# Second attention of a vision tower: q and k projected two images ahead among the scores, dense products dealt out over the body

## The reference, cut to what matters

```
n        = layernorm(x)
q, k, v  = n @ in_proj_w.T + in_proj_b          # 16 heads of 16 columns
a1       = softmax(q @ k.T / 4)                 # per head, 257 x 257
q2, k2   = n @ Qp_w.T, n @ Kp_w.T               # 64 columns
a2       = softmax(q2 @ k2.T / 8), all but the 51 largest of each row set to 0,
           and the row rescaled
v2       = n @ Vp_w.T + Vp_b
z        = n + sigmoid(lam) * (a1 @ v) @ out_proj_w.T + (1 - sigmoid(lam)) * a2 @ v2
```

## Time and profile before

| | us |
|---|---|
| median of 3 runs | 1485.66 (1483.26 to 1487.25) |
| the profiled execution | 1477.99 |
| its span | 1476.2 |
| mean granted TensorE clock | 0.832 |
| PE busy over the span | 1118.4 (76%) |
| VectorE busy over the span | 765.7 (52%) |
| second attention: first turned scores of image 0 | 661.24 |
| same, of image 7 | 1039.38 |

### The profile page before, as it was taken

The page is one execution under the profiler, slowest core; times in us unless marked ns, Lnnn a source line. Parts: engine busy times, 40 slices in busy tenths (PEclk is TensorE's granted clock), DMA queues, the critical chain, the costliest instruction groups (busy, mean ns, idle before and its releaser), DMA issues. The chain is left out here.

```text
span 1476.2 us, 21690 instructions
## 1 busy us (share of the span) xinstructions
PE 1118.4 (76%) x6799; PEld 807.9 (55%) x6799; DVE 765.7 (52%) x1788; ACT 384.5 (26%) x951; POOL 452.8 (31%) x527
## 2 busy tenths in 40 slices
PE   0358886750999990359999999999734999779888
PEld 0257774650677660235665665665422899646555
DVE  8955663230122224445556556656512377578885
ACT  0333331000222220114333334333210444222221
POOL 5941010117000007511202202211000577456665
PEclk9989998555899995667779769878657899989999
DMA  6016000102121113144314315414031200000000
GB/s 217 2 41 216 0 0 1 54 15 100 55 64 58 60 48 99 36 77 95 85 34 105 84 32 105 96 37 90 18 74 37 101 0 0 1 1 14 14 7 22
DMA packets 53403, 81.06 MB, mean 55 GB/s; under 512 B 8544, under 2 KB 45736, under 8 KB 52176
## 3 DMA queue, kind: packets, MB, share of 16 engines
q1 hardware_dynamic: 50128, 71.71, 19.1%
q0 software_dynamic: 3200, 8.43, 1.8%
HBM read 52.23 MB, written 27.62 MB: 54 GB/s over the span
## 5 line engine op out<-in xcount | busy, mean ns | idle before, releaser
L1933 DVE TENSOR_REDUCE fa_nm<-fa_ps 128x2 f32<-128x514 f32 x128 | 82.9, 690 | 74.4 <-PE fa_ps L2154 73.6
L1292 PE MATMUL ex_ps<-we_raw,ex_xT 128*128 x320 | 118.3, 494 | 0.0
L1773 ACT ACTIVATE fa_eT<-fa_ps 128x512 f32<-128x512 f32 x128 | 73.6, 590 | 81.7 <-PE fa_ps L2207 80.3
L1086 POOL DMA_INDIRECT ex_got<-y_rows,ex_pos_i x34 | 32.1, 943 | 196.9 <-DMA y_rows<-ex_y 186.8
L2945 PE MATMUL qf_ps<-qf_wg,qf_xT 128*128 128x352 f32 x272 | 89.9, 480 | 2.1 <-ACT qf_xT L2786 1.4
L2154 PE MATMUL fa_ps<-fa_ks,fa_qs 64*128 64x258 f32 x256 | 71.4, 408 | 15.4 <-DMA fa_ks<-fa_qk_rows 10.8
L447 PE MATMUL tk_ps<-tk_u,tk_qb 64*32 64x64 f32 x1024 | 22.8, 266 | 71.4 <-POOLq L314 59.7
L2207 PE MATMUL fa_ps<-fa_qs,fa_ks 66*128 66x256 f32 x256 | 71.3, 373 | 6.9 <-ACT fa_eT L1773 6.9
L1219 DVE COPY ex_hT<-ex_ps 128x384 f32<-128x384 f32 x40 | 22.3, 558 | 100.1 <-PE ex_ps L1301 100.1
L2154 PEld LDWEIGHTS fa_ps<-fa_ks,fa_qs 64*128 64x128 f32 x256 | 50.7, 258 | 40.6 <-issue 23.4
L2945 PEld LDWEIGHTS qf_ps<-qf_wg,qf_xT 128*128 128x128 f32 x272 | 50.6, 194 | 37.3 <-issue 6.6
(11 more groups left out here) (435 smaller groups left out, 2509.3 us busy)
## 6 DMA issues: line engine op xcount, KB each, us to landing
we_raw<-in_L_ffn_W SPq DMA_DIRECT2D x24, 384.0 KB
fa_qs<-fa_qk_rows SPq DMA_DIRECT2D x16, 514.0 KB
fa_ks<-fa_qk_rows SPq DMA_DIRECT2D x32, 257.0 KB, 9.9
x_rows<-tk_zero SPq DMA_DIRECT2D x1, 5120.0 KB, 19.1
ex_xin<-x_rows SPq DMA_DIRECT2D x40, 128.0 KB
y_rows<-ex_y SPq DMA_DIRECT2D x40, 128.0 KB, 1.7
fa_rsb<-fa_rs_rows SPq DMA_DIRECT2D x8, 528.0 KB
fa_qk_rows<-fa_qhl SPq DMA_DIRECT2D x32, 128.5 KB
```

The source lines that it names most:

```text
L1086: g.indirect_dma_start(out=got[0:n, a, t, :], out_offset=None, in_=y_rows[:, :], in_offset=bass.IndirectOffsetOnAxis(ap=pos_i[0:n, a, t:t ...
L1292: last = mm(ps[:, bank + t % 2, 0:HD], xT[:, t % 2, k, :], raw[:, ds(e, 1), m, k * HD:(k + 1) * HD], start=(k == 0), stop=(k == KC - 1))
L1773: cp(eT[:, j % 8, :], ps[:, ST + j % 2, :], ACT.Exp).then_inc(z["e_ready"], 1)
L1933: nc.vector.tensor_reduce(nm[:, :, j], ps[:, b:b + 2, 0:TOK], AX.X, ALU.max, negate=True).then_inc(z["max_done"], 1)
```

## The change

- q and k of image u+2 are projected in body u, q between heads 8 and 9 of image u+1 (slot 12), k between head 11 and head 12 (slot 16). Before, those of image u+1 opened body u. The first two images' are made ahead of the bodies. `xT` and `kblk` are doubled for this.
- heads 0 to 15 of image u+1 now lie in slots 7 to 17 instead of 10 to 17, one or two a slot, with other work between; `sparse_scores` moves to slot 14.
- `sparse_operands` goes from slot 3 to slot 0, `class_query` from 8 to 4, the quads from 4, 7, 10, 14 to 3, 5, 10, 15, the two halves of `values` from 8 and 9 to 8 and 17, `turn_rows` from 17 to 10, `turn_weights` from 13 to 14. `project(u-1)` is cut in two: its first half in slot 6, its second in slot 7, with T8 and head 0 between.
- the 14 rounds of VectorE are dealt out as 3, 2, 0, 3, 2, 1 over slots 0 to 5 and one each in slots 8, 9 and 11.
- the score banks are handed out by turn (`TURN`), which now has q, k and the sparse operands in it.
- SyncE's queue is reordered: the strips of image u+2 go out in body u (q before the sums, k between `sums_in` and `shares_out`), those of image u+1 are read at the start of body u, and `values_out` comes last.
- GpSimd's and ScalarE's lists follow; `E2c` and `WKc` now share the memory of `E2` and `WK`.

```diff
-    ROUNDS_AT = {0: 2, 2: 2, 3: 2, 4: 2, 5: 2, 6: 1, 7: 2, 8: 1}
-    TURNED_AT = {0: (0,), 1: (1,), 2: (2, 3), 3: (4,), 4: (5,), 5: (6,), 6: (7, 8), 7: (9,), 8: (10,), 9: (11,), 10: (12,),
-                 11: (13,), 12: (14,), 13: (15,)}
-    HEADS_AT = {10: (0, 1), 11: (2, 3), 12: (4, 5), 13: (6, 7), 14: (8, 9), 15: (10, 11), 16: (12, 13), 17: (14, 15)}
+    ROUNDS_AT = {0: 3, 1: 2, 3: 3, 4: 2, 5: 1, 8: 1, 9: 1, 11: 1}
+    TURNED_AT = {0: (0,), 1: (1,), 2: (2, 3), 3: (4, 5), 4: (6, 7), 7: (8,), 8: (9, 10), 9: (11,), 11: (12,), 12: (13,), 13: (14,),
+                 14: (15,)}
+    HEADS_AT = {7: (0,), 8: (1, 2), 9: (3, 4), 10: (5,), 11: (6, 7), 12: (8,), 13: (9, 10), 14: (11,), 16: (12, 13), 17: (14, 15)}
+    TURN = {n: i for i, n in enumerate(("operands", "class", 0, 1, 2, 3, 4, 5, 6, 7, 8, "q", 9, 10, "sparse", 11, "k", 12, 13, 14, 15))}
...
-            def body(u, p, more):
+            def body(u, p, more, two):                       # SyncE
                 if more:
-                    strips_out(u + 1, 1 - p, 0, 0, "qh_ready", "q_out", "q_in")
-                    strips_out(u + 1, 1 - p, 0, 1, "ql_ready", "q_out", "q_in")
-                    strips_out(u + 1, 1 - p, 1, 0, "kh_ready", "k_out", "k_in")
+                    strips_in(u + 1, 1 - p, 0, "q_out", "q_in")
                 max_rows(u, p, 1)
                 if more:
-                    strips_out(u + 1, 1 - p, 1, 1, "kl_ready", "k_out", "k_in")
-                    strips_in(u + 1, 1 - p, 0, "q_out", "q_in")
                     strips_in(u + 1, 1 - p, 1, "k_out", "k_in")
                     class_values(u + 1, 1 - p)
                     class_scores(u + 1)
                     sparse_class_values(u + 1, 1 - p)
-                    values_out(u + 1, 1 - p)
+                if two:
+                    strips_out(u + 2, p, 0, 0, "qh_ready", "q_out", "q_in")
+                    strips_out(u + 2, p, 0, 1, "ql_ready", "q_out", "q_in")
+                if more:
+                    max_rows(u + 1, 1 - p, 0)
                 sums_out(u, p)
                 sums_in(u)
-                if more:
-                    max_rows(u + 1, 1 - p, 0)
+                if two:
+                    strips_out(u + 2, p, 1, 0, "kh_ready", "k_out", "k_in")
+                    strips_out(u + 2, p, 1, 1, "kl_ready", "k_out", "k_in")
                 shares_out(u)
                 shares_in(u)
+                if more:
+                    values_out(u + 1, 1 - p)
...
+            def body(u, p, first, more, two):                # GpSimd
+                low_maxima(u, 1)
                 if not first:
                     shared_context(u - 1, 1 - p)
                 share_weights(u, 0)
+                if more:
+                    low_maxima(u + 1, 0)
+                if two:
+                    base(u + 2)
+                share_weights(u, 1)
+                if two:
+                    low_parts(u + 2, p)
+                    class_blocks(u + 2, p)
                 if more:
                     class_values(u + 1, 1 - p)
...
                 for sl in range(SLOTS):                      # VectorE
+                    if sl == 4 and more:
+                        class_max(u + 1, 1 - p)
+                    if sl == 13 and two:
+                        high_queries(u + 2, p)
+                    if sl == 17 and two:
+                        high_keys(u + 2)
+                    if sl == 14 and more:
+                        sparse_max(u + 1, 1 - p)
+                    if more:
+                        for j in HEADS_AT.get(sl, ()):
+                            head_max(u + 1, 1 - p, j)
+                    if sl == 7 and not first:
                         add_attention(u - 1)
+                    if sl == 8 and not first:
                         statistics(u - 1)
                     if sl == 8 and more:
+                        values(u + 1, 1 - p, 0)
+                    if sl == 11 and more:
+                        high_maxima(u + 1, 0)
+                    if sl == 17 and more:
+                        high_maxima(u + 1, 1)
+                        values(u + 1, 1 - p, 1)
                     for _ in range(ROUNDS_AT.get(sl, 0)):
+                        next_round()
                 shares(u)
...
             def projected(u, p, j, name):                    # TensorE
                 pe.wait_ge(z["x_taken"], u + 1)
                 if not isinstance(u, int) or u:
-                    pe.wait_ge(z["max_done"], N * u + j - 1)
+                    if j == 0:
+                        pe.wait_ge(z["max_done"], N * (u - 1) + 8)
+                    else:
+                        pe.wait_ge(z["e2_ready"], u)
...
-            def head_scores(u, p, j):
+            def head_scores(u, p, j, two):
...
+                elif j == 10 and two:
+                    pe.wait_ge(z["q_taken"], KC * (u + 2))
+                elif j == 13:
                     pe.wait_ge(z["e2_ready"], u + 1)
+                    if two:
+                        pe.wait_ge(z["k_taken"], KC * (u + 2))
                 else:
-                    pe.wait_ge(z["max_done"], N * u + (j - 1 if j != 10 else 10))
+                    pe.wait_ge(z["max_done"], N * u + {9: 9, 10: 9, 11: 11, 12: 12}.get(j, j - 1))
...
-            turn_class_probs(0)
-            for j in range(N):
-                head_scores(0, 0, j)
-                if j == 9:
-                    sparse_scores(0)
-                    turn_maxima(0, 0, True)
-            turn_rows(1)
+            class_query(0, 0)
+            values(0, 0, 0)
+            turn_class_probs(0)
+            turn_rows(1)
+            for j in range(N):
+                if j == 9:
+                    projected(1, 1, 0, "q_ps")
+                if j == 11:
+                    sparse_scores(0, 0)
+                if j == 12:
+                    projected(1, 1, 1, "k_ps")
+                head_scores(0, 0, j, True)
+            turn_maxima(0, 0)
+            values(0, 0, 1)
             staged(pe, body)
```

More of the change, by code:

```diff
@@ L2282, in body @@
                     if sl == 1:
[L2283 removed]
+                        turn_maxima(u, 1)
                     if sl == 2:
                         class_keys(u, p)
[L2286 to L2293 removed]
@@ L2300, in body @@
+                    if sl == 6 and not first:
+                        project(u - 1, 1 - p, 0)
+                    if sl == 14:
+                        turn_weights(u, more, two)
+                    if sl == 14 and more:
+                        sparse_scores(u + 1, 1 - p)
+                    if sl == 15:
+                        quad(u, p, 3)
+                        turn_class_weights(u)
+                    if sl == 15 and more:
+                        turn_maxima(u + 1, 0)
                     if sl == 15:
@@ L2310, in body @@
-                    if sl == 17 and two:
+                            head_scores(u + 1, 1 - p, j, two)
+                    if sl == 12 and two:
+                        projected(u + 2, p, 0, "q_ps")
+                    if sl == 7 and not first:
+                        project(u - 1, 1 - p, 1)
+                    if sl in (8, 9, 11, 12, 13):
+                        for j in TURNED_AT[sl]:
+                            turned_scores(u, p, j)
+                    if sl == 8 and more:
+                        values(u + 1, 1 - p, 0)
```

350 lines of the change are left out of this document (173 added, 177 removed).

## The result

The changed kernel takes 1619.51 us (median of 4 runs, 1611.56 to 1626.72) where the kernel before takes 1486.12 beside it (1483.26 to 1487.25): ratio 1.0899, 95% interval 1.0838 to 1.0961, slower by 133 us. Forecast were 1509 and a range to 1536. The sign was right, the size short by 110 us.

The account below looks back on a forecast made before the run. TensorE was taken to bound the kernel, partly at half clock. A steady body of 57.9 us against 54.4 gave +17.5 over five, with the edges +23.5 on 1485.7: 1509 us, range 1464 to 1536.

Parts of the forecast that it names:

- A: From a body's first turned scores (T0) to project's first half: 16.0 us, 14.4 of it from reciprocal to project.
- B: The two halves of project with a turned score and head 0: 7.6 us at full clock, up to 3 more.
- C: From project's end to the end of the one-column products: 20.7 us of work, 24.8 with waits and a turn.
- D: k, four heads and half of values, up to the next body's first turned scores: 8.0 us, 5.3 at full clock.
- clock lost in the idle time: Low clock after the idle time before project: 1.5 us a body, between 0 and 4.0.
- That is a length nothing in the change shortens: In A, 14.4 us from reciprocal to project, read from the last body, where no strips compete.
- The rule of order: In A, descriptors of one queue start in order on an engine: only k strips could delay the shares, ending at 17.
- I take no wait: In B, head 0 isn't held by the reads of q and k, landing at 17 to 24; up to 3 us possible.
- the wait drops the clock each time: Rival: idle before project drops the clock in every body; bodies of 64.8 us, 1542 us in all; chance 0.12.
- C's waits for VectorE: In C, heads 5 and 9 wait for maxima behind VectorE's rounds: 1.3 and 2.1 us.
- The edges: Outside the steady bodies: start +9, body 0 -3, body 6 -1, body 7 +1 us.

Follow-up runs that it names:

- the kernel with 14 fillers: 14 spare matmuls ahead of head 0 in the changed kernel with four-way broadcast, early shares, early q and late rounds in slot 5: 1481.96 us.
- the kernel with all moves and small reads: Changed kernel with four-way broadcast, early shares, early q and moved rounds, images 2 to 7 reading a sixteenth of q and k: 1494.29 us.
- the four-way kernel: Changed kernel with the broadcast of the shares issued as four transfers instead of one: 1559.03 us, ratio 1.0524.
- the rounds alone: Changed kernel with only the three rounds of slots 8, 9 and 11 moved to slot 5: 1597.09 us, ratio 1.0755.

## Why the prediction was wrong

Forecast and measured, in us (averages over bodies 1 to 5 of the profile after, the last column from body 4 of the kernel with 14 fillers, less these):

| step | forecast | bounds given | measured | at full clock, no waits |
|---|---|---|---|---|
| A, T0 to `project` | 16.0 | 14.9 to 19 | 23.7 | 11.6 |
| B, `project` with T8 and head 0 | 7.6 | to 10.6 | 18.1 | 7.8 |
| C, to k | 24.8 | 20.7 to 27 | 27.5 | 19.7 |
| D, to the next T0 | 8.0 | 5.3 to 9.7 | 6.6 | 5.7 |
| clock lost in the idle time | 1.5 | 0 to 4.0 | in B and C | 0 |
| body | 57.9 | | 76.0 | 44.8 |

- **The work was counted right.** 11.7, 7.6, 20.7 and 5.3 us at full clock stand against 11.6, 7.8, 19.7 and 5.7. Nothing in the size of the error comes from there.
- **A failed first, in "That is a length nothing in the change shortens".** True, but something lengthens it: 9.9 us from issue to GpSimd became 16.4. The upper bound of 19 named the reads and took the value "near the row without competitors". In the last body, where no q and k are read, the chain was as forecast: 14.3 us from the reciprocal (1187.25) to `project` (1201.57). In the kernel before, at T0 + 3, the reads were still some 13 us away; in the new order they are issued within 3 us of the broadcast. With them held, A is 17.5, within the bounds.
- **The rule of order.** I drew from the Trainium skill's "DMA: Bandwidth & Descriptors" (Two DMAs through the same engine are not ordered), which has the descriptors of one queue start in order on an engine, that by it only what was issued ahead could delay the shares, with A at 17. The trace does not bear out what I drew: transfers issued behind it on the same queue took the broadcast from 10.5 to 16.4 us, and its packets from 0.22 to 0.38 us each. Having started first did not protect it.
- **B failed in "I take no wait".** The earlier trace rows gave 13 to 16 us for the reads, with no broadcast beside them. Issued at T0 + 5.8 together with a broadcast that needs 10, they are in at T0 + 34, not at 17 to 24. The right sum was at hand: 10 + 16 us of transfers behind T0 + 4.6, one after the other, end at T0 + 31, and with the reads held it was T0 + 31.3. The two waits of body 2 are 15.2 us, and the kernel with all moves and small reads has B at 7.9.
- **The low clock was under-priced.** B's work ran at half throughout: 14.8 us instead of 7.6 in body 2. The rival "the wait drops the clock each time" had the mechanism and, with 1542, the wrong size, since it took a wait of 4 us. In the four-way kernel 16 fillers in the wait for k buy back 27 us and bring head 0 no earlier. Here the Trainium skill's "TensorE: Matmul & The Clock Gate" (HAM oscillation), by which work behind a wait starts at the low clock, agrees with the trace: 0.50 from 817.0 to 833.8, which takes in most of the wait of 11.72 us and of the first half of `project` behind it.
- **C's waits for VectorE were right in size, by the time of the kernel:** 22 us by the rounds alone, against 3.4 a body in six bodies. That C took 27.5 instead of 24.8 goes with the clock: it was 25.3 in bodies 1 and 4, at 0.76, and 30.7 in body 3, at 0.64. And where the waits come depends on A: the same rounds in slot 5 cost 26.8 us once A and B were short.
- **D was right within its range, its reason half right:** in bodies 1, 2 and 4 the one-column products ran at full clock and left it there, and D was 5.7. In body 3 the clock was at half ahead of them (D 7.5); in body 5 it was full in them and fell 0.8 us behind them (D 8.6).
- **The edges.** The start was forecast as +9 and came as +9.9. Body 0 was forecast as -3 and came as +7.2: head 0 waited 4.33 us for k, and the clock was 0.64. Body 6 was forecast as -1 and came as +21, the same error as in the others.

By ratios to the kernel before, the steps add up so: four-way broadcast, early shares, early q and moved rounds take it from 1.0899 to 1.0182, 106 us; dense work in the wait that is left, to 1.0015, 25 us more. So nearly all of the 133 us is accounted for, and most of it in the order and form of transfers. But the four-way broadcast helps the kernel before too. Against that kernel (0.9901) the best form of the change (1.0015) is still 17 us slower, and no run here makes the change pay. Not settled is what the plan could do with k and the sums in time and the rounds well placed; no kernel here reached 44.8 us a body on average. The prediction's own estimate for the kernel before without half clock was 45.9. By these two estimates, dealing the dense products out is worth a microsecond a body at equal clock, and the whole plan lived on holding the clock.

## What to carry to other kernels

Before moving a stage, list the transfers that must end between two fixed points and add their lengths: a gap that PE's work used to cover is also the gap that DMAs used to cover. A large read moved to within a few microseconds behind a small broadcast that somebody waits for slows it, though it stands behind it in the queue. And waiting on TensorE is paid again in the clock behind it: filling 45 us of waits for k won 27 to 31 in one kernel here, filling 20 us won 25 to 30 in another. So moved dense work is to lie in the waits, not between them. Last, try a repair on the kernel before too, or its gain is put down to the change.

## What the runs showed of the hardware

A broadcast of four rows to 128 partitions (528 KB) took 10 us from issue to use as one transfer, and with 256 KB of values beside it the core moved 94 GB/s. As four transfers of 32 partitions it took 3 us from the last issue, and the core moved 243 GB/s in 2 us of it. It was worth 15 us in the kernel before, for five lines.

The products of one column can run at full clock. Window of body 2 after, which holds them (870.93 to 873.41) and answers the earlier trace rows:

```profile
865.00:879.07 14.07, 12.99 (x133) 8.73 (x133) 5.25 (x10) 5.68 (x16) 3.17 (x4) 1.00 0.16 44
```

They took 2.5 us there, against 3.3 at half clock in the earlier trace rows: so they are not the same at either clock, as the prediction had it. Behind them the clock stayed full in bodies 1, 2 and 4 of this kernel, but in body 5, and in bodies 0, 3 and 5 of the kernel with 14 fillers, it fell 0.7 to 1.0 us after their end, and in body 4 of the kernel before as they began (at 923.4). What decides this isn't shown.
